# Expert layers of a hybrid transformer block that route in quarters, with statistics, result rows, blank slots and half of the first weights moved into earlier stages

## The reference, cut to what matters

```python
x = x + attention(layernorm(x))      # 2 x 2048 tokens, D = 128, 16 heads of 8
x = x + ffn(layernorm(x))            # expert layer 0
x = x + scan(layernorm(x))
x = x + ffn(layernorm(x))            # expert layer 1, same weights

def ffn(x):                          # S = 4096 tokens, E = 16 experts, C = 256 places each
    gate = softmax(x @ Wg); idx = argmax(gate, axis=1); gates_s = gate[idx]
    onehot = one_hot(idx, E)
    loc = sum((cumsum(onehot, axis=0) - 1) * onehot, axis=1)   # place in the expert's queue
    valid = loc < C
    dispatched[idx, min(loc, C)] = x                           # scatter of rows
    h = relu(einsum('ecm,emf->ecf', dispatched, w1))           # F = 512
    expert_out = einsum('ecf,efm->ecm', h, w2)
    return expert_out[idx, min(loc, C - 1)] * (gates_s * valid)
```

## Time and profile before

| what | us |
|---|---|
| median of 3 runs | 1867.91 (1867.3 to 1871.65) |
| the profiled execution, own time | 1867.34 |
| its span, first to last instruction | 1865.6 |
| `attend` | 69.7 to 946 |
| `project_out` | 947 to 960.4 |
| expert layer 0, up to its first product on fetched slots | 961.3 to 1044.9 |
| expert layer 0, experts | 1044.9 to 1124.8 |
| scan stages | 1124.8 to 1697.1 |
| expert layer 1, up to its first product on fetched slots | 1698.4 to 1782.7 |
| expert layer 1, experts | 1782.7 to the end |

### The profile page before, as it was taken

How to read it: one execution, slowest core, us unless ns; L and a number is a source line. 1 busy time by engine, 2 the same in 40 slices (tenths; PEclk the granted TensorE clock), 3 DMA queues, 4 the chain that set the end, 5 groups by cost and what they waited for, 6 DMA issues and landing times. The chain is left out here.

```text
span 1865.6 us, 42502 instructions
## 1 busy us (share of the span) xinstructions
PE 1571.6 (84%) x13842; PEld 1017.4 (55%) x13842; DVE 1381.2 (74%) x2511; ACT 962.1 (52%) x2341; POOL 658.4 (35%) x494
## 2 busy tenths in 40 slices
PE   4599998999999999999954584899999999975266
PEld 3233333333333333333343474899999999965166
DVE  6789998998998999899643134688888888865222
ACT  4167777777777777777731112344444444431011
POOL 5500000000000000000024440988888888833534
PEclk9689999999999999999975797999999999986589
DMA  3300000000000000000028403011112221104640
GB/s 106 103 19 14 17 20 21 18 12 21 19 19 12 19 20 19 13 19 20 2 102 271 136 30 97 19 50 45 45 45 51 51 45 45 45 12 157 236 121 25
DMA packets 82118, 99.92 MB, mean 54 GB/s; under 512 B 12109, under 2 KB 65482, under 8 KB 81681
## 3 DMA queue, kind: packets, MB, share of 16 engines
q1 hardware_dynamic: 76816, 85.36, 15.6%
q0 software_dynamic: 5120, 12.26, 1.8%
HBM read 43.01 MB, written 31.85 MB: 40 GB/s over the span
## 5 line engine op out<-in xcount | busy, mean ns | idle before, releaser
L566 DVE TENSOR_REDUCE chunk_max<-ps_max 128x1 f32<-128x512 f32 (+3 forms) x1280 | 705.2, 605 | 89.0 <-PE ps_max L671 64.5
L615 ACT ACTIVATE probs<-ps_s 128x512 f32<-128x512 f32 (+3 forms) x1280 | 612.8, 536 | 202.1 <-PE ps_s L663 145.0
L1434 POOL TENSOR_TENSOR lane_products<-L,q 128x1024 f32<-128x1024 f32 x176 | 411.7, 2378 | 116.6 <-POOLq L1241 47.6
L644 PE MATMUL ps_s<-Qs,Ks 50*128 50x512 bf16 (+3 forms) x1280 | 375.7, 353 | 29.7 <-DVE chunk_max L566 12.5
L654 PE MATMUL ps_max<-Ks,Qs 48*128 48x512 bf16 (+3 forms) x1280 | 384.3, 359 | 13.4 <-POOL a_ident L508 10.6
L717 PE MATMUL ps_o<-probs,Vp 128*32 128x512 f32 (+3 forms) x2560 | 343.3, 563 | 3.5 <-ACT probs L615 0.4
L644 PEld LDWEIGHTS ps_s<-Qs,Ks 50*128 50x128 bf16 x1280 | 109.4, 93 | 372.6 <-DVE chunk_max L566 311.9
L523 POOL TENSOR_TENSOR A_b<-A_newton,b_tile 128x128 f32<-128x128 f32 x32 | 14.7, 458 | 798.5 <-ACT A_newton L618 798.5
L1483 DVE TENSOR_TENSOR weighted<-exp_scores,psV_s 128x2048 f32<-128x2048 f32 x88 | 197.0, 2280 | 0.0
L1576 PE MATMUL psZT<-ident,weighted 128*128 128x128 f32 x1408 | 167.2, 274 | 1.8 <-DVE weighted L1483 1.8
L1576 PEld LDWEIGHTS psZT<-ident,weighted 128*128 128x128 f32 x1408 | 158.0, 141 | 2.0 <-DVE weighted L1483 2.0
(11 more groups left out here) (222 smaller groups left out, 2297.7 us busy)
## 6 DMA issues: line engine op xcount, KB each, us to landing
m_w<-in_L_ffn_w_dram SPq DMA_DIRECT2D x32, 512.0 KB
dispatched<-m_blank SPq DMA_DIRECT2D x2, 4128.0 KB
m_blank<-dispatched SPq DMA_DIRECT2D x16, 516.0 KB
L<-q SPq DMA_DIRECT2D x16, 448.0 KB
Qs<-q_parts SPq DMA_DIRECT2D x192, 32.0 KB
Ks<-k_parts SPq DMA_DIRECT2D x192, 32.0 KB
L<-q SPq DMA_DIRECT2D x20, 192.0 KB
L<-q SPq DMA_DIRECT2D x28, 128.0 KB
```

The costliest lines, as they stand in the source:

```text
L566: nc.vector.tensor_reduce(out, scores[:, 0:w], axis=AX.X, op=ALU.max).then_inc(max_reduced, 1)
L615: nc.scalar.activation(dst, ps_s[(k + r) % R][:, q0:], ACT.Exp, scale=SCALE).then_inc(exp_done, 1)
L644: last = nc.tensor.matmul(ps_s[(k + r) % R][:, q0:], K[r][rows, kt * P:(kt + 1) * P], Q[r][rows, g * QW + q0:(g + 1) * QW], start=True, st ...
L1434: return nc.gpsimd.tensor_tensor(out[:, l].rearrange("p (j m) d -> p j m d", m=LA), c.L[ch][:, :, l * LW:(l + 1) * LW].unsqueeze(2).broadc ...
```

## The change

It has seven parts.

- **Blank slots**: the 4.1 MB tile `blank` goes; `attend` fills one row of 258 elements and sends it 256 slots at a time from SP, once per head (32 DMAs of 264 KB), for both expert layers at once. SP waits for it (`blank_made`) ahead of the first head's loads. All blank slots now carry the token number N.
- **Weights**: w1 of experts 0 to 7 (2 MB) is loaded once, at the head of SP's stream in `attend`, and kept for both layers. A layer loads the other 6 MB, w2 first.
- **Constants** of the layers (`weight`, `token`, `up_to`, `ones`, `restart`) are made once by POOL in `attend`, behind the bias add.
- **Statistics** (`bn_stats`) of the tiles are taken by DVE in `project_out` and `scan_outputs`, chunk by chunk behind the add.
- **Result rows** are sent by SP from `project_out` (8 DMAs of 256 KB) and `scan_outputs` (4 of 512 KB); the stage now ends only when they have landed.
- **Quarters**: the layer routes 8 tiles at a time. `route` is split into `choose` (up to `onehot`) and `assign` (from the totals on); the second half's normalising stands between them. POOL's copies are in four.
- **PE's order**: `turn_tokens(ch)` is followed directly by `gate(ch)`; the counting products of quarters 0 and 1 stand behind chunk 3, and both counting products cover one quarter only, whose totals DVE adds to those of the quarter ahead. ACT loads its table for the root at once.

Cut to its core, the diff reads:

```diff
@@ attend, SP
+            for e in range(0, KEPT, 2):
+                sp.dma_start(c.w1[:, e:e + 2, :], w1[e:e + 2, :, :].rearrange("e m f -> m e f")).then_inc(w1_loaded, 16)
+            sp.wait_ge(blank_made, 2)
+            blank_slots(0)
             load(0, 0, 0, 0)
             load(1, 0, 1, 1)
...
                     load(s + 2, *following(*following(j, r)), p)
+                blank_slots(s)
@@ attend, POOL, behind its wait for made
+            nc.gpsimd.memset(c.blank[:], 0.0).then_inc(blank_made, 1)
+            pool.wait_ge(blank_made, 1)
+            nc.gpsimd.memset(c.blank[:, D:D + 1], float(N)).then_inc(blank_made, 1)
             nc.gpsimd.tensor_tensor(c.X[:], c.X[:], c.bo_rows[:].unsqueeze(1).broadcast_to([P, NT, D]), ALU.add)
+            nc.gpsimd.memset(c.restart[:], 1.0).then_inc(moe_made, 1)
...
@@ project_out
+        @block.sync
+        def _(sp):
+            for ch in range(NCH):
+                tokens = slice(ch * TC, (ch + 1) * TC)
+                sp.wait_ge(y_done, ch + 1)
+                sp.dma_start(routed.rearrange("(j p) d -> p j d", p=P)[:, tokens, :], c.X[:, tokens, :])\
+                  .then_inc(filled, 16)
+            sp.wait_ge(filled, 16 * NCH)
...
-            dve.wait_ge(y_done, NCH)
+                dve.wait_ge(y_done, ch + 1)
+                for t in range(ch * TC, (ch + 1) * TC):
+                    nc.vector.bn_stats(c.st[:, t:t + 1, :], c.X[:, t:t + 1, :]).then_inc(stats, 1)
@@ moe, POOL
-            nc.gpsimd.memset(blank[:], 0.0).then_inc(blank_made, 1)
...
-            pool.wait_ge(blanked, 16)
-            for half in range(2):
+            for q in range(QUARTERS):
...
@@ moe, DVE
-            for j in range(J):
-                nc.vector.bn_stats(st[:, j:j + 1, :], X[:, j:j + 1, :]).then_inc(stats, 1)
...
-            dve.wait_ge(made, 10)
+            dve.wait_ge(made, 1)
             normalise(0)
             normalise(1)
-            route(0)
-            route(1)
+            choose(0)
+            assign(0)
+            choose(1)
+            normalise(2)
+            assign(1)
+            choose(2)
+            normalise(3)
+            assign(2)
+            choose(3)
+            assign(3)
@@ moe, PE
-            turn_tokens(0)
-            for ch in range(NCH):
-                if ch + 1 < NCH:
-                    turn_tokens(ch + 1)
+            for ch in range(2 * CQ):
+                turn_tokens(ch)
                 gate(ch)
-                if ch == NCH - 3:
-                    count(0)
+            count(0)
             count(1)
+            for q in range(2, QUARTERS):
+                for ch in range(q * CQ, (q + 1) * CQ):
+                    turn_tokens(ch)
+                    gate(ch)
+                count(q)
```

More of the change, by code:

```diff
@@ L21 @@
 NEWTON = (15 / 8, -10 / 8, 3 / 8)
+E_ = 16
+F = 512
+CAP = (N + E_ - 1) // E_
+ROW = D + 2 + D
+QUARTERS = 4
+JQ = NT // QUARTERS
+KEPT = E_ // 2
 class Steps:
@@ L781, in _, with project_out @@
             combine(NH - 1, GP - 1)
-def project_out(nc, c):
+def project_out(nc, c, routed):
     TC = 4
@@ L852, in moe @@
     FT = F // P
-    JH = J // 2
-    HALF_STEPS = 15
+    CQ = NCH // QUARTERS
+    TRASH = 2 * N
+    FRONT_STEPS = 5
+    FIRST_STEP = [FRONT_STEPS + 15 * q + max(0, q - 1) for q in range(QUARTERS + 1)]
     with ExitStack() as cx:
@@ L981, in _ @@
             steps = Steps(dve, steps_done)
-            for j in range(J):
-                nc.vector.bn_stats(st[:, j:j + 1, :], X[:, j:j + 1, :]).then_inc(stats, 1)
-            dve.wait_ge(stats, J)
-            finish_stats(nc, steps, st, tmp, mean[:], var[:])
+            finish_stats(nc, steps, c.st, tmp, mean[:], var[:])
             dve.wait_ge(std_done, 1)
             steps.then(nc.vector.reciprocal(rstd[:], std[:]))
-            def normalise(half):
-                for ch in range(half * NCH // 2, (half + 1) * NCH // 2):
-                    for i in range(TC):
-                        j = ch * TC + i
-                        nc.vector.tensor_scalar(rows[:, j, 0:D], X[:, j, :], mean[:, j:j + 1], rstd[:, j:j + 1],
-                                                ALU.subtract, ALU.mult).then_inc(xs_ready, 1)
@@ L996, in route, with normalise @@
-            def route(half):
-                tiles = slice(half * JH, (half + 1) * JH)
-                per_token = [P, JH, E_]
-                dve.wait_ge(logits_in_psum, (half + 1) * NCH // 2)
-                steps.then(nc.vector.tensor_reduce(best[:, tiles], logits[half], axis=AX.X, op=ALU.max))
+            def normalise(q):
+                for j in range(q * JQ, (q + 1) * JQ):
+                    nc.vector.tensor_scalar(rows[:, j, 0:D], X[:, j, :], mean[:, j:j + 1], rstd[:, j:j + 1],
+                                            ALU.subtract, ALU.mult).then_inc(xs_ready, 1)
@@ L1002, in route, with choose @@
+            def choose(q):
+                tiles = slice(q * JQ, (q + 1) * JQ)
+                per_token = [P, JQ, E_]
+                dve.wait_ge(logits_in_psum, (q + 1) * CQ)
+                steps.then(nc.vector.tensor_reduce(best[:, tiles], logits[q], axis=AX.X, op=ALU.max))
                 best_b = best[:, tiles].unsqueeze(2).broadcast_to(per_token)
-                steps.then(nc.vector.tensor_tensor(work[:, tiles], logits[half], best_b, ALU.is_equal))
-                nc.vector.tensor_tensor(expd[:, tiles], logits[half], best_b, ALU.subtract).then_inc(slots_ready, 1)
+                steps.then(nc.vector.tensor_tensor(work[:, tiles], logits[q], best_b, ALU.is_equal))
+                nc.vector.tensor_tensor(expd[:, tiles], logits[q], best_b, ALU.subtract).then_inc(slots_ready, 1)
@@ L1012, in route, with assign @@
-                steps.then(nc.vector.tensor_tensor_scan(out=earlier[half][:].rearrange("p e j -> p (e j)"),
-                                                        data0=restart[half][:].rearrange("p e j -> p (e j)"),
-                                                        data1=totals[half][:].rearrange("p e j -> p (e j)"), initial=0.0,
+            def assign(q):
+                tiles = slice(q * JQ, (q + 1) * JQ)
+                mine = onehot[:, 1 + q * JQ:1 + (q + 1) * JQ, :]
+                dve.wait_ge(counted, q + 1)
+                if q:
+                    steps.then(nc.vector.tensor_tensor(totals[q][:, :, 0], totals[q][:, :, 0], earlier[q - 1][:, :, JQ - 1],
+                                                       ALU.add))
+                steps.then(nc.vector.tensor_tensor_scan(out=earlier[q][:].rearrange("p e j -> p (e j)"),
+                                                        data0=c.restart[:].rearrange("p e j -> p (e j)"),
+                                                        data1=totals[q][:].rearrange("p e j -> p (e j)"), initial=0.0,
@@ L1624, in _, with scan_outputs @@
             chunks(pe, section)
-def scan_outputs(nc, c):
+def scan_outputs(nc, c, out):
     with ExitStack() as cx:
@@ L1636, in scan_outputs, with _ @@
         psY = [ps(f"psY_o{u}") for u in range(2)]
-        gated, gT_in_psum, gT_copied, y_in_psum, y_done = (
-            sem(n) for n in ("gated", "gT_in_psum", "gT_copied", "y_in_psum", "y_done"))
+        gated, gT_in_psum, gT_copied, y_in_psum, y_done, stats, filled = (
+            sem(n) for n in ("gated", "gT_in_psum", "gT_copied", "y_in_psum", "y_done", "stats", "filled"))
         block = cx.enter_context(nc.Block())
+        @block.sync
+        def _(sp):
+            for ch in range(SC):
+                sp.wait_ge(y_done, ch + 1)
+                sp.dma_start(token_rows(out, ch), c.X2[:, ch]).then_inc(filled, 16)
+            sp.wait_ge(filled, 16 * SC)
         @block.gpsimd
```

188 lines of the change are left out of this document (96 added, 92 removed).

## The result

| us | before | after |
|---|---|---|
| median of the runs (lowest to highest, number) | 1869.78 (1867.3 to 1874.59, 4) | 1887.83 (1880.1 to 1888.89, 4) |
| the profiled execution | 1867.34 | 1880.1 |

The ratio after to before is 1.0081, with a 95% interval of 1.0064 to 1.0098: the change makes the kernel slower, where the forecast was 1856.7. Executions of one kernel lie up to 9 us apart. Much of that is attention, whose 31 heads behind head 0 took 808.0 to 817.4 us in the profiles of this study, and just as much in the eleven of them in which nothing in attention was changed. So I compare stretches, and times only as ratios.

What follows compares the result with a forecast made beforehand. POOL's row of 32 scatters was taken as the bound. Terms -23.8 + 4.6 + 3.2 + 4.8 = -11.2 us against 1867.34 gave 1856.1, or 1856.7 as the median of runs; range 1850 to 1866.

Steps and rivals of the forecast that it cites:

- What bounds the kernel: Expert layers: all engines wait for POOL's 32 scatters, a fixed 40.6 us; only their start can be moved.
- Term 1: Expert layers: first scatter 24.8 us after the block's start instead of 37.7; net -11.9 us a layer, -23.8 for both.
- Does POOL run through?: Expert layers: later quarters' PE and DVE cycle of 10.1 us keeps up with POOL's 10.15; DVE costs POOL 1.0 a layer.
- Rival 1: Expert layers: the cycle is longer than POOL's row, chunks 4.0 us; 3 us lost a layer, 1862.7; chance 0.12.
- Rival 2: Expert layers: DVE gets one normalising instruction through per scatter, eight take 10.2 us; slower, 1874.1; chance 0.08.
- Rival 4: Expert layers: POOL waits in full for each of 16 normalising instructions; 4.3 us more a layer, 1865.3; chance 0.09.
- Rival 5: Expert layers: quarters don't bring the scatter forward, four chunks still precede the first count; 1861.9; chance 0.06.
- Rival 3: Stage ends and attention's start: landings cost nothing extra; -1.5, -1.6 and -1.5 us, 1852.1; chance 0.10.
- Term 2: Ends of `project_out` and `scan_outputs`: statistics and landing of result rows delay the expert layers by 4.6 and 3.2 us.
- Term 3: Attention's start: head 0's loads queue behind weights and blank slots, PE starts at 82.7; +4.8 us after a cheaper cast.
- Terms of zero: Blank slots within attention's heads, POOL's constants, the layers' 6 MB of weights and the experts: no cost.
- Sum: Whole kernel: all terms give -11.2 us against the profiled execution's 1867.34, so 1856.1.

Runs made afterwards that it cites:

- e9_xs: The changed kernel, but for chunks 4 to 7 VectorE normalises into a separate tile, which TensorE turns and ScalarE copies into `rows`; ratio to before 0.9955.
- e10_best: e9_xs with loads of heads 0 and 1 first, GpSimd's copies after 16 normalised tiles, next chunk turned ahead of each gate; 1842.3 us, ratio to before 0.9842.
- e4_head: The changed kernel with loads of heads 0 and 1 first, weights and blank slots behind head 2's loads; head 0's end at 139.08 us against 144.80.
- e2_probe: The kernel before plus 16 rounds of TensorE turning tiles of `rows` and ScalarE copying them beside the scatters; rounds 1.80 us, then 4.6, 4.9, 9.1 and 5.6.

## Why the prediction was wrong

- **What bounds the kernel: right.** The row of 32 scatters at 1.27 us is what everything waits for, and moving its start moves the layer's end when the row isn't broken (e9_xs against before: first scatter 11.2 us earlier, first turn of slots 11.1 and 11.7 us earlier).
- **Term 1, first scatter: 26.6 instead of 24.8.** Too small was the head, 6.5 instead of 4.9 us and outside its bounds. I let only normalising instructions wait for POOL's copy and took the steps of the statistics as before; four of them wait. The Trainium skill (SBUF — State Buffer, section "SBUF: two separate sides") says that an instruction of VectorE with two SBUF inputs and a GpSimd instruction that reads SBUF exclude each other for their whole length; the trace agrees for L61 to L63, 0.93 to 1.06 us beside the copies and 0.19 to 0.21 without (e10_best); L64, with one input, waited as well (0.95). The four chunks (3.50 us each) and count to first scatter (6.1) came as summed.
- **"Does POOL run through?" is the step that failed.** Its cycle is right where nothing holds PE up: in e9_xs count follows count after 10.2 us (forecast 10.1), and quarter 3 is ready 4 us ahead of its turn. DVE's normalising cost POOL nothing and took 2.14 us a group, not 4.1. What failed in the changed kernel is its term "two chunks 7.0", which took PE's work beside the scatters to cost what it costs ahead of them: the turn of chunk 7 was held up by 14 and 17 us, so the last count followed the one before it after 24.8 and 27.1 us instead of 10.1, and POOL waited 11.46 and 13.93 us for quarter 3. In the kernel before no row of PE lies between 1003.6 and 1044.9, while POOL scatters until 1039.7; an operation that the trace doesn't show in that company should have had a bound of its own. It was worth 24.2 us: 1880.1 against 1855.9 in the profiled executions of after and e9_xs, and counted from the blocks' starts the last scatters of the two layers come 11.2 and 13.7 us earlier there. Rival 1 had the doubt ("every number in it comes from a row made under another order") but not the size, and the sign that I gave for rivals 1 and 2, a gap on a DVE releaser, came (`m_rows` L1059) although neither was the cause: DVE passed on what PE had lost.
- **Rivals.** Rival 2 named the slower side with the wrong mechanism: eight normalising instructions took 2.14 us beside the scatters, not 10.2. Rival 4 fell: scatters kept 0.96 us and a pitch of 1.27 us beside DVE. By the rule of the Trainium skill that the prediction set beside it (DMA: Bandwidth & Descriptors, section "SWDGE vs HWDGE vs iDMA"), VectorE in its 2-port mode locks GpSimd out of its descriptor rings; the trace shows no loss of POOL's of this kind, and whether the normalising instructions run in that mode no run here tells. Rival 5 fell, the scatters did come forward. Rival 3's cheap landings didn't come.
- **Term 2: right** (+3.8 for 4.6; +3.2 for 3.2). The adds' pitch was 1.50, not 1.58.
- **Term 3: 6.2 for 4.8.** PE started at 83.95 instead of 82.7; the cast did get cheap (0.17 us at 90.94). e4_head shows the term's cause.
- **Terms of zero: right for attention's heads** (808.4 us for 31 of them against 808.0). The experts got 1.4 and 1.6 us shorter, which I haven't explained.
- **Sum.** Without the hold-up the changed kernel's profiled execution is 1855.9 (e9_xs) where the sum gave 1856.1. That closeness is in part luck: this execution is the fastest of five, whose median is 1862.31, and the ratio of 0.9955 makes it 8.4 us less than before, not 11.2; and a longer head of the layer and of attention was offset by a POOL that lost nothing and by shorter experts.

## What to carry to other kernels

Price an operation by a row that stands in the same company as the one to come; if the trace has none (here PE beside a long row of scatters), the bound is open upwards, and a probe in the old kernel can show it in one run, as e2_probe did. Where TensorE stands still beside a long row of indirect transfers, try another pitch for the tile that it reads: padding `rows` from 1032 to 1088 bytes took the ratio from 1.0081 to 0.9957, some 23 us, here. Keep GpSimd's copies away from VectorE's short two-input steps on a critical path.

## What the runs showed of the hardware

- TensorE, reading tiles 1032 bytes apart, was held up by up to 7.3 us a round in the probes, and by 14 and 17 us at the changed kernel's chunk 7, from 16 to 21 us into an unbroken row of scatters at 1.27 us (DMA share 0.29), and was free again 0.6 to 4.2 us after the last scatter of it. Pauses of 1.8 us after every eighth scatter prevented it; with pitches of 512, 1040 and 1088 bytes it didn't come.
- ScalarE and VectorE in turn showed no long round beside the same row: 1.35 us with both on PSUM, up to 1.28 us with VectorE reading `rows`. ScalarE's writes into `rows` took 0.62 us.
- The Trainium skill (SBUF — State Buffer, section "SBUF: two separate sides") states that engine ports and DMA ports can't contend and that TensorE waits for nobody there. The probes show a hold-up of TensorE by the row of scatters; that it happens at SBUF's ports they don't show, and where it sits stays open.
